# Gate and up columns of the first block in chunks of 512, 512 and 352 instead of 460, 460 and 456

## The reference

```python
def _L0_attn_ref(x, w_gate, w_up, w_down):        # x 4x512x512, I = 1376
    s = silu(einsum('bsh,ih->bsi', x, w_gate))
    k = int(0.5 * I)
    _, idx = top_k(-abs(s), k)                      # the k smallest |s| of each token become 0
    s = s with those set to 0.0
    s = s * einsum('bsh,ih->bsi', x, w_up)
    return einsum('bsi,hi->bsh', s, w_down)

x = x + layernorm(_L0_attn_ref(layernorm(x), w_gate, w_up, w_down))
x = x + layernorm(_L0_ffn_ref(layernorm(x), W_gate, W_up, W_down))   # the same without the selection
```

## Time and profile before

| | |
|---|---|
| median of 3 runs | 838.15 us (836.0 to 840.37) |
| the profiled execution's own time | 837.27 us |
| its span, first to last instruction | 835.5 us |
| mean granted TensorE clock | 0.974 |
| busy: PE, PE weight load | 778.4 us (93%), 652.6 us (78%) |
| busy: DVE, ACT, POOL | 396.8 us, 321.1 us, 195.0 us |
| bytes moved | 51.18 MB, 61 GB/s in the mean |

### The profile page before, as it was taken

One profiled execution on the slowest core, in us unless ns is written; L12 is line 12 of the kernel. 1 busy time (PEld: TensorE's weight loads), 2 busy tenths in 40 slices (PEclk: granted clock), 3 DMA queues, 4 the chain that ended last, 5 costly groups with the idle time before them and its releaser, 6 DMA issues.

```text
span 835.5 us, 9714 instructions
## 1 busy us (share of the span) xinstructions
PE 778.4 (93%) x3568; PEld 652.6 (78%) x3568; DVE 396.8 (47%) x756; ACT 321.1 (38%) x478; POOL 195.0 (23%) x518
## 2 busy tenths in 40 slices
PE   5857997999999999999788699999999999999996
PEld 4756886888888888888677588788887888788884
DVE  6665554656556765555768234133221532232113
ACT  6655453555564555554553122121211311121112
POOL 1453343333434443344410000020000200020002
PEclk9978999999999999999899799999999999999999
DMA  8600067011111101111450400101010210012001
GB/s 277 216 1 1 26 209 248 26 39 39 38 39 39 39 1 39 38 39 40 159 186 26 160 13 14 38 35 55 13 51 1 89 38 0 1 51 75 1 1 50
DMA packets 22050, 51.18 MB, mean 61 GB/s; under 512 B 2160, under 2 KB 5488, under 8 KB 21808
## 3 DMA queue, kind: packets, MB, share of 16 engines
q1 hardware_dynamic: 22000, 50.54, 17.9%
HBM read 42.14 MB, written 16.84 MB: 71 GB/s over the span
## 4 chain that ended last, share of the span: by engine, by line
PE 77%; DVE 6%; DMA 5%; POOL 4%; ACT 4%; issue 2%; SPq 1%; DVEq 0%; POOLq 0%; ACTq 0%
PE gu_ps L427 29%; PE gu_ps L377 20%; PE tr_ps L448 11%; PE y_ps L406 10%; PE y_ps L448 4%; DMA xin<-in_L_attn_x 3%; ACT junk L527 3%; PE tr_ps L391 2%; POOL thr L1046 1%; DMA stage<-in_L_attn_w_gate 1%; POOL move L1043 1%; PE gu_ps L359 1%; DVE absv L761 1%; POOL err L1041 1%; PE tr_ps L359 1%
## 5 line engine op out<-in xcount | busy, mean ns | idle before, releaser
L527 ACT ACTIVATE junk<-absv,thr 128x1376 bf16<-128x1376 f32 x96 | 138.5, 1443 | 172.1 <-POOL thr L1046 118.6
L864 DVE TENSOR_TENSOR prod<-gu_ps,prod 128x512 f32<-128x512 f32 (+1 forms) x44 | 30.4, 691 | 187.3 <-PE gu_ps L427 187.3
L377 PE MATMUL gu_ps<-gate_hi,xT 128*128 128x460 f32 (+1 forms) x384 | 114.2, 379 | 0.0
L377 PE MATMUL gu_ps<-up_hi,xT 128*128 128x460 f32 (+1 forms) x384 | 113.4, 377 | 0.0
L406 PE MATMUL y_ps<-down_hi,hT 128*128 128x512 f32 (+1 forms) x352 | 112.8, 402 | 0.0
L377 PE MATMUL gu_ps<-gate_lo,xT 128*128 128x460 f32 (+1 forms) x192 | 74.5, 388 | 14.7 <-DVE prod L770 12.9
L377 PEld LDWEIGHTS gu_ps<-gate_hi,xT 128*128 128x128 f32 x384 | 74.6, 194 | 8.0
L406 PEld LDWEIGHTS y_ps<-down_hi,hT 128*128 128x128 f32 (+1 forms) x352 | 68.3, 194 | 15.6
L377 PEld LDWEIGHTS gu_ps<-up_hi,xT 128*128 128x128 f32 x384 | 73.8, 192 | 8.0
L572 ACT ACTIVATE prod<-gu_ps 128x512 f32<-128x512 f32 (+1 forms) x44 | 26.3, 598 | 139.7 <-PE gu_ps L427 139.7
L406 PE MATMUL y_ps<-down_lo,hT 128*128 128x512 f32 (+1 forms) x176 | 71.3, 405 | 8.1 <-DVE hT L740 8.1
(11 more groups left out here) (112 smaller groups left out, 1414.1 us busy)
## 6 DMA issues: line engine op xcount, KB each, us to landing
xin<-x_scratch SPq DMA_DIRECT2D x18, 256.0 KB, 2.7
xin<-in_L_attn_x SPq DMA_DIRECT2D x16, 256.0 KB, 2.8
xres<-in_L_attn_x SPq DMA_DIRECT2D x16, 256.0 KB, 2.9
x_scratch<-xres SPq DMA_DIRECT2D x16, 256.0 KB, 2.0
xres<-x_scratch SPq DMA_DIRECT2D x14, 256.0 KB, 2.9
out<-xres SPq DMA_DIRECT2D x14, 256.0 KB, 2.0
raw<-in_L_ffn_W_gate SPq DMA_DIRECT2D x1, 2752.0 KB, 11.8
raw<-in_L_ffn_W_up SPq DMA_DIRECT2D x1, 2752.0 KB, 20.8
```

The lines of the kernel that those rows point to most:

```text
L377: last = nc.tensor.matmul(dst[:, 0:CW[n]], xt, w, start=(c == 0 and i == 0), stop=(c == KC - 1 and i == 2))
L527: nc.scalar.activation(junk[:, :], absv[:, j % 2, :], ACT.Sign, bias=thr[:, j % 2:j % 2 + 1], scale=-1.0, accum_out=sgn[:, j % 2:j % 2 + 1 ...
L864: nc.vector.tensor_tensor(prod[0:k, 0, GW:2 * GW], bank(("u", idx, 0))[0:k, :], prod[0:k, 0, 0:GW], ALU.mult).then_inc(p2_done, 1)
```

## The change

Two lines of constants. The three chunks of the gate and of the up columns are 512, 512 and 352 wide, where they were 460, 460 and 456; their sum stays 1376. The number of matmuls, of activations, of DVE operations and of DMAs, and their order on every engine, stay as they are: only the widths of the instructions that `CW` and `CO` feed change (`product`, `silu`, `times_up`, and the first 12 weight pieces in `load_w`, `split_weights_hi` and `split_weights_lo`).

```diff
-    CW = [460, 460, 456]
-    CO = [0, 460, 920]
+    CW = [512, 512, 352]
+    CO = [0, 512, 1024]
```

## The result

The changed kernel takes 840.70 us in the median of 20 runs, the kernel before 837.28 us in the median of 20 on the same chips. The ratio is 1.0035, 95% interval [1.0024, 1.0046]: 0.35% or some 2.9 us slower, where 3.1 us and 0.37% had been forecast (the two medians by themselves are 3.4 us apart, 0.41%). By a bound of 0.5% this is the same; the interval alone lies wholly above 1.

What follows compares the result with a forecast made beforehand. TensorE was taken to set the pace in steady tiles, with serial chains at the start and block change. Terms 0 + 2.5 + 0.8 + 0.1 - 0.3 = +3.1 us on 838.15 gave 841.2 us, range 838.1 to 843.4.

Steps and rivals of the forecast that it cites:

- The cover of h: Steady tiles: G2, cut to 1.97 us, no longer covers the 2.28 us to hT; 0.31 us wait, eight times, +2.5 us.
- The columns: Gate and up matmuls of a tile: 48 widened ones cost +1.04 us, 24 narrowed ones -1.04 us, net 0.0.
- the constant of 17.4 ns: First-block matmuls: each costs its columns at 2.4 GHz plus 17.4 ns, giving 230.7 ns at 512 and 164.1 at 352.
- The rival on short matmuls: Gate and up chunks: 352-column matmuls take 147 to 150 ns, G2 1.79 us, wait 0.49 us; 842.7 us, chance 0.07.
- The weight load: Rival, narrow chunks: weight loads keep 352-column matmuls at 208 ns, no wait, 1.04 us more per tile; 847 us, chance 0.08.
- The serial places: At 97.24 and 371.43 us, where TensorE gives way to a serial chain: abs 0.4 us later at each, +0.8 us.
- The prologue: Start of the kernel: larger early weight pieces delay U2 by 0.3 us, narrower U2 and silu save time; -0.3 us.
- The signs: Changed profile: windows 24.6 us, G2 1.97 to 2.03, G0 and G1 5.48 to 5.57, abs 3.15 after G2, U2 near 28.9.
- The row "PE y_ps L406 <- DVE hT L740": Sign in the list of waits: TensorE waits for hT in 8 or 9 tiles, about 0.2 to 0.3 us each.
- The stretch at 113.67: Sign in the chain: the prediction is wrong if this stretch moves by more than a microsecond.
- part 2: Steady tiles: the wait for hT behind narrow G2, +2.5 us, range 2.0 to 2.5; with the column costs 1.2 to 3.1.
- part 1: Matmul columns of a tile: widened and narrowed chunks cancel, 0.0 us, bounds -0.11 to +0.07 a tile.

Runs made afterwards that it cites:

- experiment 3: Changed kernel, but ACT makes the high parts of h before silu(j, 0) in tiles 2 to 15; 835.64 us, ratio 0.9973 to the kernel before.
- 7: Changed kernel with the narrow chunk first, 352, 512, 512 for gate and up; ratio 1.0000 to the kernel before.
- 5: Changed kernel with silu(j, 1) also ahead of the high parts of h, so hT comes later; single run, 845.90 us.
- 1: Kernel before with only the gate chunks at 512, 512, 352, up left at 460, 460, 456; ratio 1.0042.
- 2: Kernel before with only the up chunks at 512, 512, 352, gate left at 460, 460, 456; ratio 0.9983.
- experiment 8: Kernel before with chunks of 484, 484 and 408, halfway to the changed kernel; ratio 0.9999.
- experiment 6: Kernel before with silu(j, 1) also ahead of the high parts of h, old widths kept; single run, 838.93 us.
- experiment 4: Kernel before with the high parts of h ahead of silu(j, 0), old widths kept; ratio 0.9992.

## Why the prediction was right

**The cover of h** was the step that decided, and it held: none of the other theories gives 24.65 with the narrow G2, 24.27 with the same widths when hT is early (experiment 3), 24.25 when the narrow chunk stands elsewhere (7), 25.15 when hT is later still (5), and a growth that comes with gate alone (1, 2). The change did not make any engine do more. It took 0.58 us (2.49 to 1.91) from a chunk behind which 2.25 to 2.29 us of serial work on ACT and DVE had to fit.

**Its size.** Foreseen 0.31 us a tile and 0.0 from the columns; measured 24.65 - 24.27 = 0.38 and 24.27 - 24.31 = -0.04, together 0.34. Both terms were off a little and against each other. Eight windows: 2.76 us by the second loads, foreseen 2.5.

**The columns.** 512 columns cost 232.3 ns ((13.06 - 1.91) / 48, from the pieces of 60 and of 12 matmuls in experiment 3) and 352 cost 159 ns, foreseen 230.7 and 164.1. The step that was wrong is the constant of 17.4 ns on top of the columns: it is 19 at 512, 17 at 460 and 12 at 352. That shortened G2 by another 0.06 us, which all went into the wait. The rival on short matmuls had the direction right, a 352-column matmul pays less, but not the size (it had 0 to 3 ns on top). For matmuls by themselves, the Trainium skill's N/2.4 + 2.5 ns (TensorE: Matmul & The Clock Gate, Back-to-back issue gap) would be 215.8 and 149.2; the trace is above it at both.

**The weight load** does not set the distance: two loads in 0.35 us at a distance of 0.16, each recorded with 0.19, overlap.

**The serial places.** Abs begins 249.53 - 246.43 = 3.10 us after G2's start, foreseen 3.15, before 3.27. G0 and G1 together are 24 x 23.3 = 0.56 us longer. So abs comes 0.39 later at each of the two places, foreseen 0.4. The two traces give nearly that: from the start of the up chunks before (80.98 and 79.68) to abs (97.83 and 96.90) 0.37 us more, and from the second load of the ninth `down` (346.93 and 347.32) to abs (372.01 and 372.81) 0.41 more. That this is worth 0.8 in the end is not shown by a run of its own.

**The prologue.** The last silu of tile 1 starts at 38.56 in place of 38.91, and the counting behind it at 38.93 in place of 39.35, -0.42, foreseen -0.3. U1 of tile 0 starts at 25.93 and not at 25.00, U2 at 28.88, foreseen 28.9. By the traces of experiments 1 and 2 it is the sum of two larger parts, +1.1 of gate and -1.2 of up. That the sum came out so near is partly luck, since the end of G2 alone moves by some 0.3 us among traces with the old widths.

**The signs.** Windows, abs and U2 of tile 0 came out as foreseen. G2 in 1.91 us lies just under its 1.97 to 2.03, and G0 and G1 in 5.58 (24 x 232.3 ns) just above 5.57. The row "PE y_ps L406 <- DVE hT L740" for 8 or 9 tiles is not in the list, which has 3 such waits as before. By its letter that was a sign of being wrong; the wait itself is there, under the weight loads. The stretch at 113.67 starts at 112.73, 0.94 us earlier, and is 1.3 us shorter, so what stands behind it comes 2.3 us earlier: by its start it is just inside the microsecond, by its end outside. The prologue gives 0.4 of this; the most comes from the first `down`, at a higher clock, and the load of x, which the change doesn't explain.

**Slips in the working.** It is four pieces of each matrix that become larger, not the first eight; the sum of 4288 counts them rightly. The lower end of part 2 with part 1 is 1.1 and not 1.2. The forecast is given as +2 in the list of chances, and as 839.6, +1.5, in the range after it. And 0.3% of 838 is 2.5 us, so with the scatter of single executions its range would be 837.1 to 844.9, not 838.9 to 843. The forecast time also stands on a median of three, 838.15, which is 0.9 above the median of 20. The rival on short matmuls is priced wrong: what G2 saves only turns into wait, and the narrow up chunk's 0.17 us are a gain, so with 352 columns at 149 ns and 512 as forecast a tile would grow by 0.31 - 0.17 = 0.14 us, less than the forecast and not 0.49. The rival takes 512 as cheap too and lets the sum stay, but against the measured 209 ns of 460 columns that sum would fall. None of this moves the time that was forecast or the cause.

**What one trace doesn't give.** The two profiled executions differ by 1.4 us in span, the medians by 3.4. The load of x behind the copies took 27.49 us and not 28.81. The first `down`, partly at half clock, took 9.32 and not 10.06 (granted clock 0.83 and 0.77). U0 and U1 of tile 15 took 5.59 and not 6.57 (1.00 and 0.74). In the second block, which the change doesn't touch, the first two chunks took 7.21 and not 5.71 (0.78 and 1.00). These four are -1.3, -0.7, -1.0 and +1.5, in all -1.5; without them the traces would differ by 2.9 us, as the ratio says. The load also scatters among kernels with the old widths, 27.69 in experiment 6 and 28.33 in experiment 4. That the other three go with the clock is read from the granted clock in the traces, and I made no run for it.

## What to carry to other kernels

When a matmul group stands between a producer and its consumer on TensorE, its length is a cover: read how long the way over the other engines takes from the group's start, and compare the two, before changing tile widths that leave the sum alone. If a narrow remainder is needed, place it where nothing is being prepared behind it, and put what TensorE will wait for first in the other engine's queue; here this turned +0.35% into -0.27%. In a prologue fed by pieces, look at the last pieces that the consumer waits for: with up's made smaller, the start took 1.2 us less in the trace.

## What was not expected of the hardware

The time that a matmul takes above its columns at 2.4 GHz is not a constant: 12 ns at 352, 17 at 456 and 460 and 19 at 512 columns, all with the same operands in the first block. It does not simply grow with the width either: in experiment 8 it is 16 ns at 408 and at 484 (186 and 218 ns apart). In the second block, with weights and activations exchanged, it is 15 at 512. Why, these runs don't tell.
